# Long convolutions of a decoder layer: filter taps laid out in pairs 16 steps apart, and four buffer loads per slice in place of six

## The chip, the cores and the metric

The kernel runs on one core of a Trainium2 chip. The metric is the device time of one execution in microseconds. PE is the matrix engine, DVE the vector engine, ACT the scalar engine, POOL the general engine, SP the engine that issues most transfers.

## The reference

One decoder layer for 8 sequences of 256 tokens, width 256. Its first block makes q, k and v by projections, a 4-tap convolution and SiLU, runs a chunked delta rule with inverted triangles of 32x32, and mixes five paths per head with a gate. Three of the paths are causal depthwise convolutions of v with 3, 15 and 64 taps:

```
def _dwconv(x, w):
    K = w.shape[1]
    xt = jnp.pad(jnp.transpose(x, (0, 2, 1)), ((0, 0), (0, 0), (K - 1, 0)))
    y = jax.lax.conv_general_dilated(xt, w[:, None, :], (1,), 'VALID',
        dimension_numbers=('NCH', 'OIH', 'NCH'), feature_group_count=w.shape[0])
    return jnp.transpose(y, (0, 2, 1))
paths = jnp.stack([_dwconv(v, fir_s), _dwconv(v, fir_m), _dwconv(v, fir_l), delta_path, v], axis=3)
```

(reshapes left out). A cross attention over a second input and a mixture of experts follow; each block ends in a residual and a layer norm. All arrays are float32.

## The kernel before

The phase `phase_project_invert_and_fir` does, for 8 batches in a software pipeline (`weave`), the projections (L423), the short convolutions (ACT L499, DVE L550), the transposes (L456), norms (DVE L567, POOL L594 and L597, DVE L574) and the triangle matrices. Each engine's program is an order written out by hand; semaphores tie them. At its end come the long convolutions (`pe_fir`, `act_fir`), beside DVE's inversion of the triangles (`dve_invert`).

**How a long convolution becomes a product.** Channels are cut into 8 slices (`SLICES`) of 32 channels (`SL`). For one channel, `win` holds windows of 128 time steps of v, one for each of the 32 blocks of 64 outputs (8 batches x 4 blocks). The buffer `hank` holds for each of 3 filters (`NF`) and each of 64 steps (`BLK`) the filter shifted by that step, over 128 partitions. The product of L666 takes the 128x32 windows of one channel as weights and streams the 3 x 64 = 192 columns of `hank` for that channel. There are 256 such products, four at a time on four column groups (`q`) of the array. Each shows as two records in the trace (512), since the data are float32. Two channels (`u`) of each of the four groups make a `pair`; ACT copies a pair out of PSUM to `stage` in one instruction (L686), turned so that channels lie innermost. A slice has four pairs.

**The layout.** The buffer is `hank[k, f, s, c]`, so the columns of one channel lie 32 floats (128 bytes) apart. It is filled from a DRAM copy of the transposed filters, `rt_dram[slice, f, n, c]`, with `hank[k, f, s, c] = rt[f, k + s, c]`: partition k reads one run of consecutive rows from row k. Only ranges in which taps can be nonzero are loaded, in six transfers per slice (the tuple `HANK`, function `sp_hank`, L763 to L768); the rest stays zero from a clearing by POOL at the start (L345, 12 memsets).

**Making `rt_dram`.** The filters are loaded right-aligned to the zeroed `wpad` (L312), turned by PE (L322, 6 transposes), copied by ACT (L328, 6 copies) to `filters`, and stored by SP (L336, 8 transfers, and L339 for the rows of zeros behind).

**Order of SP.** Slices 0 to 3 are loaded during rounds 4 to 7 of the batches (`sp_first_hank`), to four buffers (`RING`). Slice n from 4 to 7 is loaded when the last product of slice n - 4 is done (`sp_late_hank`). SP then goes on in this order (`sp_first`, L914 to L927): the inverses of the first half (L608, which wait for DVE), the tokens of batches 0 and 1 (L973), the triangles of batch 0 (L983, L984, which wait for the inverses in DRAM), the stage stores of slices 0 to 3 (L614), the triangles of batch 1, the stage stores of slices 4 to 7. The next phase loads the convolved paths (L1150) after all six stage stores have landed, and then tokens of batch 2 (L973).

**Order of DVE.** The first inversion, then a fixed part of the second, then the first products of the next phase (L1115), which need tokens; L1119 needs PE's transposes of L1003, which on PE stand behind the last product of L666.

Of the kernel before, what the change touches and what calls it, by code (L numbers as in the profile page):

```python
# [226 lines left out]
HANK = ((2, 1, 0, 32), (2, 1, 32, 96), (2, 1, 96, P), (0, 2, 48, 64), (0, 2, 64, 96), (0, 2, 96, P))  # L227
# [15 lines left out]
def phase_project_invert_and_fir(pg, a, env):  # L243
# [5 lines left out]
    with ExitStack() as mem:  # L249
# [10 lines left out]
        n_stage, n_inv, n_filters = NF * BLK * CH, NG * CH * CH, KT * NF * P  # L260
# [9 lines left out]
        stage = [views(r, 0, n_stage, "p (f t c) -> p f t c", f=NF, t=BLK) for r in (room0, room1)]  # L270
# [13 lines left out]
        filters = views(room3, 0, n_filters, "p (k r f c) -> p k r f c", k=KT, r=RING, f=NF)  # L284
        wpad = views(room3, n_filters, n_filters, "p (k f n) -> p k f n", k=KT, f=NF)
        am = views(room3, 0, n_inv, "p (g i j) -> p g i j", g=NG, i=CH)
        no_taps = env.hank[0][0:BLK, 0, 0:SLICES * NF, :]
# [28 lines left out]

        def pe_filters():
            pe.wait_ge(s.wpad, 16 * NF)
            for k in range(KT):
                for f in range(NF):  # L320
                    n = k * NF + f
                    m = nc.tensor.transpose(ps[:, 6 + n // 4, n % 4 * P:(n % 4 + 1) * P], wpad[:, k, f, :], ident[:])  # L322
            m.then_inc(*s.filters_turned.up())

        def act_filters():
            act.wait_ge(s.filters_turned, 1)
            for n in range(KT * NF):
                S.copy(filters[:, n // NF, :, n % NF, :].rearrange("n r (q c) -> n q r c", q=NCH),  # L328
                       ps[:, 6 + n // 4, n % 4 * P:(n % 4 + 1) * P].rearrange("n (q r c) -> n q r c", q=NCH, r=RING)
                       ).then_inc(*s.filters_copied.up())  # L330

        def sp_filters():
            sp.wait_ge(s.filters_copied, KT * NF)
# [7 lines left out]
        def pool_hank_zero():  # L341
            for h in env.hank:
                for f in range(NF):
                    pool.in_turn()
                    G.memset(h[:, f].rearrange("k s c -> k (s c)"), 0.0).then_inc(*pool.tick(env.hank_zero))  # L345
# [62 lines left out]
        def pe_project(b):  # L408
# [37 lines left out]
        def pe_normalise(b):  # L446
            for j in range(3):
# [3 lines left out]
                else:  # L451
                    pe.wait_ge(s.win_made, b)
                    pe.wait_ge(s.filters_copied, KT * NF)
# [58 lines left out]
        def act_normalise(b):  # L512
# [7 lines left out]
            act.wait_ge(s.tok_out[i], 16 * (b // 2))  # L520
            S.copy(tok[i][:, :, 2, :], ps[:, 6, :].rearrange("p (t d) -> p t d", t=TT)).then_inc(*s.v_copied.up())
# [41 lines left out]
        def dve_normalise(b):  # L563
# [7 lines left out]
            dve.wait_ge(s.tok_out[i], 16 * (b // 2))  # L571
# [187 lines left out]
def sp_hank(pg, env, sl):  # L759
# [3 lines left out]
    for f, count, k0, k1 in HANK:  # L763
# [5 lines left out]
        if k1 == P:  # L769
            yield  # L770
# [1974 lines left out]
```

## Time and profile before

| | us |
|---|---|
| median of 3 runs | 985.71 (980.92 to 992.03) |
| the profiled execution, its own time | 989.73 |
| its span in the trace | 987.9 |
| PE busy | 880.9 (89% of the span) |
| DVE busy | 605.2 (61%) |
| ACT busy | 453.4 (46%) |
| products of the long convolutions (L666), 512 records | 44.7 |

Busy times are sums over the span; matrix instructions overlap, and busy time counts the overlap once. An engine that is busy need not be the one that sets the end: for this, the stretch from 120 to 205 us has to be read, in which the long convolutions end and the next phase begins. The granted clock of PE is 0.95 of full speed on average over the span.

### The profile page before, as it was taken

How to read it: one execution, taken by the hardware profiler on the slowest of the kernel's cores; microseconds unless marked ns; L12 is line 12 of the kernel's file. 1: busy time of each engine (PE TensorE's matmuls, PEld its weight loads, DVE VectorE, ACT ScalarE, POOL GpSimd, SP SyncE). 2: the span in 40 equal slices, each digit the busy share in tenths (PEclk: the TensorE clock that was granted, in tenths of full speed). 3: DMA queues.
4: the chain of work that ended last, by engine and by line, in shares of the span. 5: the costliest groups of instructions: out<-in, count | busy, mean ns of one | idle time of the engine just before them, and what ended most of it. 6: DMA issues, size and time to landing. Idle time of an engine off the chain costs nothing.

```text
span 987.9 us, 18338 instructions
## 1 busy us (share of the span) xinstructions
PE 880.9 (89%) x6859; PEld 656.0 (66%) x6859; DVE 605.2 (61%) x1409; ACT 453.4 (46%) x845; POOL 342.9 (35%) x334
## 2 busy tenths in 40 slices
PE   7799789889999988898889888989997999999995
PEld 5667566667777766687556555656785777777774
DVE  5799798566888887452657767774462343333255
ACT  5687665446666664443144543445331322222221
POOL 9422201023556555331001343223540242222683
PEclk9899999768999997899799999999998999999998
DMA  5689769996455431121992112002302222221421
GB/s 169 186 276 276 205 169 258 285 238 152 108 116 114 82 76 54 53 86 70 387 375 93 63 63 87 11 23 87 92 23 82 65 56 64 65 67 49 150 65 64
DMA packets 144396, 123.52 MB, mean 125 GB/s; under 512 B 89718, under 2 KB 126518, under 8 KB 143030
## 3 DMA queue, kind: packets, MB, share of 16 engines
q1 hardware_dynamic: 140902, 112.98, 40.3%
q0 software_dynamic: 3408, 9.38, 2.5%
q8 instruction: 56, 0.92, 0.4%
q14 instruction: 30, 0.25, 0.1%
HBM read 74.04 MB, written 48.29 MB: 124 GB/s over the span
## 4 chain that ended last, share of the span: by engine, by line
PE 60%; DVE 13%; ACT 10%; POOL 8%; issue 4%; DMA 3%; SPq 2%; POOLq 0%; DVEq 0%; ACTq 0%; another core or an unknown queue 0%
PE ps L2498 10%; PE ps L1904 6%; PE ps L2513 5%; PE ps L666 4%; DVE cross_room L1937 4%; PE ps L2362 3%; PE ps L1844 3%; PE ps L1605 2%; PE ps L2375 2%; PE ps L1338 2%; POOL hank L345 2%; PE ps L1966 2%; POOL kept L2645 2%; PE ps L423 2%; PE ps L1489 2%
## 5 line engine op out<-in xcount | busy, mean ns | idle before, releaser
L1982 ACT ACTIVATE cross_room<-ps 128x1024 f32<-128x1024 f32 x64 | 65.5, 1023 | 99.3 <-PE ps L1908 94.8
L2498 PE MATMUL ps<-wr,xbT 128*128 x312 | 100.4, 465 | 1.8 <-ACT xbT L2534 1.8
L1937 DVE TENSOR_REDUCE cross_room<-ps 128x4 f32<-128x1024 f32 x64 | 78.0, 1223 | 38.5 <-PE ps L1904 37.7
L1904 PE MATMUL ps<-kept,cross_room 32*128 32x256 f32 x512 | 73.3, 407 | 21.7 <-DVE cross_room L1937 20.1
L2587 POOL DMA_INDIRECT y_dram<-yb,dest_row x39 | 37.4, 960 | 136.4 <-DVE dest_row L2563 132.2
L1306 POOL TENSOR_TENSOR st<-st,exponent 128x20 f32<-128x20 f32 x16 | 56.5, 3533 | 66.1 <-DVE st L1281 64.8
L2498 PEld LDWEIGHTS ps<-wr,xbT 128*128 128x128 f32 x312 | 59.3, 191 | 30.1 <-issue 3.5
L1908 PE MATMUL ps<-cross_room,kept 32*128 32x256 f32 x512 | 74.5, 409 | 0.0
L1904 PEld LDWEIGHTS ps<-kept,cross_room 32*128 32x128 f32 x512 | 46.5, 188 | 39.6 <-issue 22.9
L550 DVE SCALAR_TENSOR_TENSOR room<-room 128x256 f32<-128x256 f32 x144 | 58.3, 478 | 11.6 <-ACT room L499 11.6
L2572 DVE TENSOR_TENSOR cross_room<-cross_room,ps 128x352 f32<-128x352 f32 x39 | 20.3, 521 | 60.3 <-PE ps L2498 58.9
L2542 ACT ACTIVATE cross_room<-ps 128x352 f32<-128x352 f32 x39 | 18.1, 463 | 73.4 <-PE ps L2498 73.4
L2578 DVE TENSOR_SCALAR yb<-ps,weight 128x256 f32<-128x256 f32 x39 | 18.9, 484 | 50.5 <-PE ps L2513 50.5
L423 PE MATMUL ps<-room,weights 128*128 128x256 f32 x192 | 46.6, 395 | 3.4 <-DMA room<-in_conv_v 2.7
L666 PE MATMUL ps<-hank,win 128*32 128x192 f32 x512 | 44.7, 513 | 5.0 <-issue 2.7
L1281 DVE TENSOR_REDUCE st<-paths 128x20 f32<-128x1280 f32 x32 | 47.1, 1476 | 0.0
L1908 PEld LDWEIGHTS ps<-cross_room,kept 32*128 32x128 f32 x512 | 44.7, 188 | 1.8 <-issue 1.4
L423 PEld LDWEIGHTS ps<-room,weights 128*128 128x128 f32 x192 | 37.0, 200 | 9.1 <-DMA room<-in_conv_v 3.1
L666 PEld LDWEIGHTS ps<-hank,win 128*32 128x32 f32 x512 | 30.6, 150 | 18.2 <-issue 5.5
L2432 POOL TENSOR_TENSOR hTlo<-cross_room,hThi 128x512 fp32r<-128x512 f32 (+1 forms) x24 | 31.1, 1298 | 30.7 <-ACT hThi L2391 29.5
L1338 PE MATMUL ps<-dxT,w1x 128*128 128x256 f32 x128 | 38.2, 426 | 2.9 <-ACT stT L1362 2.9
L2362 PE MATMUL ps<-x2Thi,whi 128*128 128x512 f32 (+1 forms) x96 | 38.6, 403 | 0.6 <-issue 0.6
(350 smaller groups left out, 2253.8 us busy)
## 6 DMA issues: line engine op xcount, KB each, us to landing
xs_dram<-params SPq DMA_DIRECT2D x17, 1040.0 KB, 17.9
room<-in_gW SPq DMA_DIRECT2D x8, 1280.0 KB, 8.4
tok_dram<-room SPq DMA_DIRECT2D x8, 768.0 KB, 5.9
fir_dram<-room SPq DMA_DIRECT2D x6, 1024.0 KB, 7.2
paths<-fir_dram SPq DMA_DIRECT2D x48, 128.0 KB, 3.7
xb<-xs_dram SPq DMA_DIRECT2D x39, 130.0 KB, 2.4
hank<-rt_dram SPq DMA_DIRECT2D x8, 512.0 KB, 7.9
yr<-y_dram SPq DMA_DIRECT2D x16, 256.0 KB, 3.3
```

The source lines that it names most:

```text
L423: m = nc.tensor.matmul(ps[:, 1 + j, c * T:(c + 1) * T], W[j][:, k, c * P:(c + 1) * P], xT[:, k, :], start=(k == 0), stop=(k == KT - 1))
L550: V.scalar_tensor_tensor(out=conv[:, j, c, :], in0=raw[:, j, c, tap:tap + T], scalar=taps[:, j, c, tap:tap + 1], in1=conv[:, j, c, :], op0 ...
L666: m = nc.tensor.matmul(ps[q * CH:(q + 1) * CH, sl % 2 * PAIRS + pair, u * NF * BLK:(u + 1) * NF * BLK], win[:, sl // RING, :, q * CH + in_ ...
L1306: G.tensor_tensor(st[:, t, 3].rearrange("p n h -> p (n h)"), st[:, t, 1].rearrange("p n h -> p (n h)"), env.exponent[:, 1, 0:NPATH * H], A ...
L1338: m = nc.tensor.matmul(ps[:, 6 + c // 2, (c % 2) * T:(c % 2 + 1) * T], w, xT[:, k, :] if k < KT else stT[:], start=(k == 0), stop=(k == KT))
L1904: m1 = nc.tensor.matmul(ps[:, c, t * T:(t + 1) * T], strips(qS[b % 3], g, c)[:, t * P:(t + 1) * P], kS(b, g)[c * CH:(c + 1) * CH], start=T ...
L1908: m2 = nc.tensor.matmul(ps[:, c, t * T:(t + 1) * T], kS(b - 1, g)[c * CH:(c + 1) * CH, t * P:(t + 1) * P], strips(qS[(b - 1) % 3], g, c), ...
L1937: V.tensor_reduce(mx[:, :, g, XD + 2 * h * CH:XD + (2 * h + 1) * CH + 1:CH].rearrange("p t c -> p c t"), ps[:, pair(h), :].rearrange("p c ...
L1982: S.activation(pT[g % 2][:, pair(h)].rearrange("p c k t -> p (c k t)"), ps[:, pair(h), :].rearrange("p c n -> p (c n)"), ACT.Exp).then_inc ...
L2362: m = nc.tensor.matmul(ps[0:fn, 2 * par + j, :], w[a_][:, j, k, f0:f0 + fn], env.x2T[b_][:, k, tg * TG:(tg + 1) * TG], start=(k, a_, b_) = ...
L2498: m = nc.tensor.matmul(ps[:, 2 * (j % 2) + half, 0:FF], xbT[j % 2][:, k, :], wr[:, bass.ds(e, 1), k, half, :].rearrange("p e n -> p (e n)" ...
L2513: m = nc.tensor.matmul(ps[:, 5 + j % 2, 0:D], hbT[j % 2][0:fn, n, :], wdr[n][0:fn, bass.ds(e, 1), :].rearrange("p e n -> p (e n)"), start= ...
```

## The change

The buffer and its DRAM copy are laid out anew. A period of 32 steps (`PER`) is cut in two halves of 16 (`LAG`), and steps t and t + 16 lie side by side: `hank[k, a, f, i, c, h]` holds step `32a + 16h + i`. In DRAM a row of 64 floats holds for each of 32 channels the tap of row n and the tap of row n + 16. So a product streams 96 pairs of adjacent floats, pairs 64 floats (256 bytes) apart; the columns stay 192, in another order.

The filters are turned twice, once shifted by 16 (12 transposes, 12 copies in place of 6 and 6), and `wpad` is 16 columns wider. PE writes the turned filters to banks 6, 7 and 3 and therefore waits for the first batch's raw copies; the third projection of batch 1 waits for the copies of the filters. `filters` moves to the second token buffer, so ACT's and DVE's writes of batch 1's tokens wait for the filter stores to have landed. Rows of the filter stores are 256 bytes, not 128.

A slice is loaded in four transfers: filter 2 over partitions 32 to 127 for the first half of the steps and 0 to 95 for the second; filters 0 and 1 over 80 to 127 and 48 to 95. Every run is 4,096 bytes. `stage` is laid out as [2 halves, 3 filters, 32 steps, 32 channels], so a stage store has two runs of 4 KB per partition, not one of 8 KB, in the same six transfers. The copy of L686 moves the same 384 elements in the new order.

```diff
-HANK = ((2, 1, 0, 32), (2, 1, 32, 96), (2, 1, 96, P), (0, 2, 48, 64), (0, 2, 64, 96), (0, 2, 96, P))
+LAG = 16
+PER = 2 * LAG
+STEPS_A = BLK // PER
+HANK = ((2, 1, 0, 32, P), (2, 1, 1, 0, 96), (0, 2, 0, 80, P), (0, 2, 1, 48, 96))
...
+        def filter_bank(n):
+            return ps[:, (6, 7, 3)[n // 4], n % 4 * P:(n % 4 + 1) * P]
...
+            pe.wait_ge(s.raw_copied, 3)
+            for n in range(FILTERS):
+                h, k, f = n // (KT * NF), n // NF % KT, n % NF
+                m = nc.tensor.transpose(filter_bank(n), wpad[:, k, f, h * LAG:h * LAG + P], ident[:])
...
+                S.copy(filters[:, k, :, f, h::2].rearrange("n r (q c) -> n q r c", q=NCH),
+                       filter_bank(n).rearrange("n (q r c) -> n q r c", q=NCH, r=RING)).then_inc(*s.filters_copied.up())
...
+                if j == 2 and b == 1:
+                    pe.wait_ge(s.filters_copied, FILTERS)
...
+            if b == 1:
+                act.wait_ge(s.filters_out, FILTERS_OUT)
...
+            if b == 1:
+                dve.wait_ge(s.filters_out, FILTERS_OUT)
...
-                nc.sync.dma_start(env.fir_dram[f, c * NCH:(c + 1) * NCH].rearrange("q (n t) d -> (q n) (t d)", t=BLK),
-                                stage[c][:, f].rearrange("p t d -> p (t d)")).then_inc(*env.fir_out.up(16))
+                nc.sync.dma_start(env.fir_dram[f, c * NCH:(c + 1) * NCH].rearrange("q (n a t) d -> (q n) a (t d)", a=STEPS_A, t=PER),
+                                stage[c][:, :, NF - 1 - f].rearrange("p a t d -> p a (t d)")).then_inc(*env.fir_out.up(16))
...
-                                                 env.hank[sl % RING][:, :, :, q * SL // NCH + pair * 2 + u].rearrange("k f s -> k (f s)"),
+                                                 env.hank[sl % RING][:, :, :, :, q * SL // NCH + pair * 2 + u].rearrange("k a f i h -> k (a f i) h"),
...
-                    S.copy(stage[sl // RING].rearrange("p f t c -> p c f t")[:, c0:c0 + 2, :, ::-1],
-                           ps[:, sl % 2 * PAIRS + pair, 0:2 * NF * BLK].rearrange("p (c f t) -> p c f t", c=2, f=NF)
+                    S.copy(stage[sl // RING].rearrange("p a f (h i) c -> p c (a f) i h", h=2)[:, c0:c0 + 2, ::-1, ::-1, ::-1],
+                           ps[:, sl % 2 * PAIRS + pair, 0:2 * NF * BLK].rearrange("p (c n i h) -> p c n i h", c=2, i=LAG, h=2)
...
+    for f, count, step, k0, k1 in HANK:
+        row = 2 * SL
+        src = bass.AP(tensor=rt.tensor, offset=((sl * NF + f) * (P + BLK) + PER * step + k0) * row,
+                      ap=[[row, k1 - k0], [(P + BLK) * row, count], [1, LAG * row]])
+        nc.sync.dma_start(env.hank[sl % RING][k0:k1, step, f:f + count].rearrange("k f i c h -> k f (i c h)"),
+                          src).then_inc(*env.hank_in[sl % RING].up(16))
+        if step:
+            yield
...
-        env.rt_dram = nc.dram_tensor("rt_dram", [SLICES, NF, P + BLK, SL], F32).ap()
+        env.rt_dram = nc.dram_tensor("rt_dram", [SLICES, NF, P + BLK, 2 * SL], F32).ap()
...
-            env.hank = [mem.enter_context(nc.sbuf_tensor(f"hank{i}", [P, NF, BLK, SL], F32)) for i in range(RING)]
+            env.hank = [mem.enter_context(nc.sbuf_tensor(f"hank{i}", [P, STEPS_A, NF, LAG, SL, 2], F32)) for i in range(RING)]
```

## Rows read from the trace of the kernel before

**Rows 1.** Chain of waits, 118 to 240 us: start us, length us, what.
```profile
129.19 41.68 PE ps L666 x437
...
180.71 9.68 DMA fir_dram<-room
...
195.94 5.85 DMA delta_room<-tok_dram
```

**Rows 2.** PE groups by shape: count, busy us, mean ns of one, idle before.
```profile
L666 PE MATMUL ps<-hank,win 128*32 128x192 f32 x512 | 44.7, 513 | 5.0 <-issue 2.7 <-DVE room L584 2.3
...
L1966 PE MATMUL ps<-cross_room 128*32 128x256 f32 x512 | 35.1, 393 | 2.6 <-ACT cross_room L1982 2.6
```

**Rows 3.** Lines L666, L423, L456: ns min/median/max, first and last start us.
```profile
L666 PE MATMUL ps<-hank,win x512: 500/500/599, 120.1 to 170.4; 128*32 128x192 f32 x171
...
L423 PE MATMUL ps<-room,weights x192: 377/378/796, 7.7 to 109.5; 128*128 128x256 f32 x192
...
L456 PE MATMUL ps<-ident,room x96: 271/273/477, 19.0 to 117.2; 128*128 128x128 f32 x96
```

**Rows 4.** Stretches: length, busy of PE, PEld, DVE, ACT, POOL, clock, DMA share, GB/s.
```profile
60.00:110.00 50.00, 44.20 (x300) 34.76 (x298) 45.94 (x104) 38.86 (x77) 12.40 (x8) 1.00 1.02 284
...
138.00:162.00 24.00, 24.00 (x286) 16.73 (x282) 21.70 (x62) 18.60 (x25) 1.94 (x2) 1.00 1.03 217
162.00:167.00 5.00, 5.00 (x60) 3.41 (x56) 4.64 (x11) 2.88 (x4) 0.00 (x0) 1.00 1.02 410
...
206.97:229.70 22.73, 22.17 (x213) 17.22 (x213) 13.57 (x24) 7.49 (x21) 7.07 (x2) 0.50 0.90 203
```

**Rows 5.** Timeline of SP's transfer issues: start us, length us, line, what, count.
```profile
27.14 0.70 SPq L339 DMA_DIRECT2D rt_dram<-hank  x1
...
133.77 17.76 SPq L767 DMA_DIRECT2D hank<-rt_dram  x24
151.57 0.90 SPq L608 DMA_DIRECT2D t_dram<-room  x2
...
178.89 3.78 SPq L614 DMA_DIRECT2D fir_dram<-room  x3
```

**Rows 6.** SP's waits, 120 to 200 us: total us, times, longest us.
```profile
SPq L69 <- DMA t_dram<-room: 13.0, 1, 13.0
...
SPq L767 <- PE ps L666: 5.6, 3, 2.3
```

**Rows 7.** Timeline of DVE, 118 to 200 us: idle before and releaser in brackets.
```profile
124.17 0.91 DVE L625 MEMSET room<- 128x1024 f32 x1 [0.16 <-issue]
...
169.15 0.69 DVE L1115 TENSOR_TENSOR kept<-delta_room,beta 128x512 f32<-128x512 f32 x1 [0.37 <-DMA delta_room<-tok_dram]
172.46 0.69 DVE L1119 COPY kept<-ps 128x512 f32<-128x512 f32 x1 [2.62 <-PE ps L1003]
```

**Rows 8.** Timeline of ACT in the long convolutions.
```profile
137.60 2.69 ACT L686 COPY room<-ps 128x384 f32<-128x384 f32 x4
```

**Rows 9.** Timelines of POOL, ACT and DVE in the first 50 us.
```profile
5.75 22.30 POOL L345 MEMSET hank<- 128x2048 f32 x12
...
20.62 1.08 ACT L328 COPY room<-ps 128x128 f32<-128x128 f32 x6
...
42.65 0.56 ACT L521 COPY room<-ps 128x512 f32<-128x512 f32 x1
...
32.05 1.29 DVE L574 TENSOR_TENSOR room<-ps,room 128x512 f32<-128x512 f32 x2 [3.11 <-POOL room L597]
```

**Rows 10.** Timeline of PE at four places.
```profile
101.50 0.66 PE L404 MATMUL ps<-ident,room 128*128 128x128 f32 x4 [1.25 <-DMA room<-in_x]
...
190.06 1.14 PE L1025 MATMUL ps<-kept 64*128 64x96 f32 x16
...
201.83 0.66 PE L1003 MATMUL ps<-ident,delta_room 128*128 128x128 f32 x4 [1.01 <-DMA delta_room<-tok_dram]
...
208.12 2.03 PE L1025 MATMUL ps<-kept 64*128 64x96 f32 x16
```

More of the change, by code:

```diff
@@ L269, in phase_project_invert_and_fir @@
         xT = views(room1, n_raw + 2 * n_tok + 2 * n_x, n_x, "p (k t) -> p k t", k=KT)
-        stage = [views(r, 0, n_stage, "p (f t c) -> p f t c", f=NF, t=BLK) for r in (room0, room1)]
+        stage = [views(r, 0, n_stage, "p (a f t c) -> p a f t c", a=STEPS_A, f=NF, t=PER) for r in (room0, room1)]
         room2 = sb("room2", [P, 2 * n_inv])
@@ L283, in phase_project_invert_and_fir @@
         room3 = sb("room3", [P, n_inv])
-        filters = views(room3, 0, n_filters, "p (k r f c) -> p k r f c", k=KT, r=RING, f=NF)
-        wpad = views(room3, n_filters, n_filters, "p (k f n) -> p k f n", k=KT, f=NF)
+        filters = tok[1].rearrange("p t j d -> p (t j d)").rearrange("p (k r f c) -> p k r f c", k=KT, r=RING, f=NF)
+        wpad = views(room3, 0, n_wpad, "p (k f n) -> p k f n", k=KT, f=NF)
         am = views(room3, 0, n_inv, "p (g i j) -> p g i j", g=NG, i=CH)
-        no_taps = env.hank[0][0:BLK, 0, 0:SLICES * NF, :]
+        no_taps = views(env.hank[0][0:BLK].rearrange("k a f i c h -> k (a f i c h)"), 0, SLICES * NF * 2 * SL, "k (n c) -> k n c", n=SLICES * NF)
+        FILTERS, FILTERS_OUT = 2 * KT * NF, 16 * (KT * RING + 1)
         gw1_rows = a["gW1"][D:, :].rearrange("(n g p) c -> p g n c", n=NPATH, p=P)
@@ L326, in act_filters @@
             act.wait_ge(s.filters_turned, 1)
[L327 to L330, printed above, removed]
+            for n in range(FILTERS):
+                h, k, f = n // (KT * NF), n // NF % KT, n % NF
+                S.copy(filters[:, k, :, f, h::2].rearrange("n r (q c) -> n q r c", q=NCH),
+                       filter_bank(n).rearrange("n (q r c) -> n q r c", q=NCH, r=RING)).then_inc(*s.filters_copied.up())
         def sp_filters():
-            sp.wait_ge(s.filters_copied, KT * NF)
+            sp.wait_ge(s.filters_copied, FILTERS)
             for k in range(KT):
@@ L344, in pool_hank_zero @@
                     pool.in_turn()
-                    G.memset(h[:, f].rearrange("k s c -> k (s c)"), 0.0).then_inc(*pool.tick(env.hank_zero))
+                    G.memset(h[:].rearrange("k a f i c h -> k (a f i c h)")[:, f * BLK * SL:(f + 1) * BLK * SL], 0.0).then_inc(*pool.tick(env.hank_zero))
         def sp_first_hank(sl):
@@ L452, in pe_normalise @@
                     pe.wait_ge(s.win_made, b)
-                    pe.wait_ge(s.filters_copied, KT * NF)
+                    pe.wait_ge(s.filters_copied, FILTERS)
                 for t in range(TT):
@@ L762, in sp_hank @@
     nc, rt = pg.nc, env.rt_dram
-    for f, count, k0, k1 in HANK:
-        s0, s1 = max(0, P - FIRS[f + count - 1] - k1 + 1), min(BLK, P - k0)
-        src = bass.AP(tensor=rt.tensor, offset=((sl * NF + f) * (P + BLK) + s0 + k0) * SL,
-                      ap=[[SL, k1 - k0], [(P + BLK) * SL, count], [1, (s1 - s0) * SL]])
-        nc.sync.dma_start(env.hank[sl % RING][k0:k1, f:f + count, s0:s1, :].rearrange("k f s c -> k f (s c)"),
+    for f, count, step, k0, k1 in HANK:
[3 more added lines that the diff above has]
+        nc.sync.dma_start(env.hank[sl % RING][k0:k1, step, f:f + count].rearrange("k f i c h -> k f (i c h)"),
                           src).then_inc(*env.hank_in[sl % RING].up(16))
-        if k1 == P:
+        if step:
             yield
```

6 lines of the change are left out of this document (1 added, 5 removed).

## The prediction

> **What bounds the kernel now.** I read the chain of waits around the long convolutions first. One piece of 41.68 us, the products of L666, runs from 129.19 us to the end of the stage, and two transfers stand behind it: the stores to `fir_dram` that let SP go on at 190.4, and the token load issued then, whose landing starts products at 201.83 [rows 1], for which PE had idled 1.01 us [rows 10]. So three chains have to be separated: PE, the transfers, DVE.
>
> **PE.** A float32 product is two records in the trace. L666 streams 192 columns, 128 bytes from one to the next, and its record lasts 500 ns at the median. L423 with 256 columns side by side lasts 378, the transpose of L456 with 128 lasts 273 [rows 3]: 105 ns per 128 columns, so 192 should last 325. The excess, 175, is about a second time the 160 that 192 columns cost by this slope: the spread columns are read at half rate. L1966 has the same 128x32 weights in four column groups and 256 columns side by side: 68.6 ns of engine time per record (35.1/512) against 87.3 (44.7/512) for L666 [rows 2].
>
> **Transfers.** From 138 to 162 us the queues are full (share 1.03) and move only 217 GB/s, while in 162 to 167, where whole 128-partition loads and stores pass, they move 410 [rows 4]. In the full stretch it is the `hank` loads of slices 4 to 7: 4 x 1,444 KB = 5.91 MB at 217 GB/s is 27.3 us, from their first issue at 133.77 [rows 5] to about 161.5. SP waited for PE before three of these slices, 5.6 us in all [rows 6]. Behind them queue the inverses, issued at 151.57 when DVE has them [rows 5], and the tokens. SP then waits 13.0 us for the inverses to land [rows 6], and only then issues the triangles and the stage stores of L614, the second half at 178.89 [rows 5]. The order of SP thus makes the store wait for the last `hank` load, not for the last product.
>
> **DVE.** It inverts triangles from 124.17 to 168.8 in a fixed order, and its first work of the next phase starts at 169.15, after 0.37 us lost on the token load; then it waits 2.62 us for PE's L1003 [rows 7]. That 2.6 is all that an earlier end of L666 can give here.
>
> **The change, part by part.**
>
> *Products.* Each now reads 96 pairs of neighbours, pairs 256 bytes apart. No row has pairs. The lower bound of the time is L1966's per column, 68.6 x 192/256 = 51.5 ns per record, 26.4 us in all; the upper is no gain, 44.7. I take full rate, between 51.5 and the 68.6 that the nearest row needs as it stands [rows 2]: 26.4 to 35.1 us, so PE saves 10 to 18 us of its 44.7, and a slice takes 3.3 to 4.4 us instead of 5.6. The row that decides is the excess of 175 ns, which goes if two reads share what one pays for.
> The Trainium skill (SBUF — State Buffer, Specifications (TRN2)) says that the memory has 16-byte lines and needs two hits in a line for full bandwidth. By this rule one float in a line is slow and the pair is enough, and a record would last 325 ns. The 500 ns agree with its first half; no run here shows the second.
>
> *Late slices.* The old transfers of a slice are, from the ranges in the code, 124, 512, 128, 56, 368 and 256 KB, the 512 over 64 partitions, the others over 16 or 32; the new ones are 384 KB each, two over 96 partitions and two over 48: 1,536 KB, 6% more. Their price is unknown. All at 410 GB/s, a slice takes 3.84 us against 6.81 now, -11.9 us for four; all at 217, 7.25, +1.7. But 217 is a mean of wide and narrow: if the 64-partition load alone ran at 410 (524 kB in 1.28 us), the narrow 954 kB took 5.53, which is 173 GB/s. With the new narrow half (786 kB) at 173 and the wide half at only 217, a slice takes 4.55 + 3.62 = 8.17, +5.4 for four: the upper end. I take the wide half at 410, as 96 partitions are nearest to the full ones, and the narrow at 173: 1.92 + 4.55 = 6.47, -1.4 for four. The start moves too: faster PE frees the buffers earlier, and slice 5, for which SP waited on PE, can be issued some 2 us earlier. Of this I count 1.5, since slice 4 stays where SP puts it, at 133.77. Last load: 2.9 us earlier, about 158.6.
> By the Trainium skill (SBUF — State Buffer, Door 1: The DMA port swizzle) a transfer within 32 or 64 partitions reaches half of the ports. An estimate from its table gives the old slice 1.7 times the time per byte of full width, near the 410/217 = 1.9 of the rows, and the new one 1.5 to 1.7: by it four slices take 2.2 us less to 0.8 more, and the gain below would be 0.8 to 3.5.
>
> *End of the stage.* PE waits for slice 7 and does it in 3.3 to 4.4: its end moves from 171 to about 163. DVE then saves its 2.6, no more. Late next is the chain of transfers: inverses, triangles, stores of 6 MB, paths, tokens, all 2.9 us earlier. At 201.83 PE had lost 1.01 us on the tokens [rows 10]; coming 2.5 us earlier it could use them 3.5 earlier, and gets them 2.9 earlier. **Gain: 2.9 us.** Even if the transfers gave more, 2.5 + 1.0 = 3.5 is the limit here.
>
> *Evacuation.* The 32 copies of L686 keep 384 elements. Four in a row take 2.69, 0.67 each [rows 8]; against 16 x 51.5 ns = 0.82 of PE per copy, ACT is just enough, with three table loads beside it. Other strides on the write side: 0 to +0.2 us each. I take 0, as the old ones jump already 128 bytes between elements, and +0.2 x 32 = 6.4 would still end before slice 7's load; for slice 7 alone it is +0.8. PE may run 8 copies ahead.
>
> *Stage stores.* The same 6 transfers and bytes, in pieces of 4 KB, not 8. The 410 GB/s of [rows 4] were moved mostly in 4 and 6 KB rows, so 0.
>
> *First half.* Six more transposes on PE, six more copies on ACT (1.08 for six now, at 20.62), a `wpad` memset larger by 96 columns. The copies delay the square, the DVE sum and the raw copies behind them by 1.1 us. What hides it: POOL clears `hank` until 28.05 and only then takes the sum; DVE waits 3.11 us for POOL's power [rows 9]. If the clearing were 3 us shorter, the 1.1 would be on the path. PE waits newly for these copies at batch 1's third projection, some 2 us after their end, with all later products behind it: 0. The memset is on the path: at 22.30/12 us for 2,048 columns [rows 9], 96 cost +0.1. SP issues the nine filter transfers 1.1 later, in rows of 256 bytes, not 128, and behind them the loads of a batch. They are all issued by 27.84 [rows 5], and the new waits on them, ACT's L521 and DVE's L574 of batch 1, come first at 42.65 [rows 9]: some 14 us of cover for twice the bytes, so 0. If it went, each engine would stop with the rest of batch 1 behind it. Slices 0 to 3 load beside the projections, at share 1.02 [rows 4]: by the same price -0.3 per slice, which nobody waits for but the load of `in_x` at 101.50 (1.25 us, [rows 10]); I take 0, the upper end is +1.36 per slice. SP issues two transfers less per slice, 17.76/24 = 0.74 us each with their waits [rows 5]: beside other work, 0.
>
> **Sum.** -2.9 + 0.1 = -2.8. The profiled execution took 989.73 (span 987.9 and 1.8 around it), 4.0 above the median of 985.71; its gaps are taken as the median's. 989.73 becomes 986.9, and the median 982.9: **983**.
>
> **Rivals.**
> *A, the narrow loads set the pace (slower).* Half of the new bytes go to 48 partitions,. At 8.17 us per slice the late loads end 5.4 - 1.5 = 3.9 later, the tokens at 169 and 201.83 with them, and each early slice adds up to 1.36 to a full queue: +3.9 to +9.3, 990 to 995. It decides once a slice takes over 7.2 us. For: 65% of the old bytes were narrow and made 217 of 410; against: now 50% are. Chance 0.17.
> *B, transfers relieved.* Towards 410 the last `hank` lands before the inverses leave DVE; gain 3.5 plus the 1.25 at 101.50: 981. Chance 0.15.
> *C, the pairs do nothing.* Records stay at 500 ns and PE ends as now; the transfers alone give -1.0 to +5.4: 985 to 991. For: no row has pairs. Chance 0.08.
> *D, the clock.* From 206.97 to 229.70 PE is granted 0.50, its lower level of 1.2 GHz, after it had idled [rows 4]; the sixteen records of L1025 take 2.03 us there and 1.14 a batch earlier [rows 10]. With all of its 22.7 us scaled so, the stretch costs 9.9, with nothing 0; I take 6.6, since DVE, busy for 13.6 of it, does not get faster. PE will now idle in the convolutions, waiting for loads, and a stretch may come or go: -6.6 or +6.6 with the rest, 976 or 990. Chance 0.1 each way.
> The Trainium skill (TensorE: Matmul & The Clock Gate, HAM oscillation) says that stalls between bursts of products put the engine back to the slow clock; by it the new idle time would sooner cost a stretch, the 990 above.
>
> The forecast itself has 0.4, with 980 to 987 as its own range. Together, low 975 (B with D) and high 993 (most of A). A measurement here tells about 1% (9.9 us) from no change. Faster by that needs B and D together, -3.5 - 1.3 - 6.6, or luck in both medians: 0.15. Slower by that, A with D: 0.11. Within: 0.74.
>
> **What would show it.** Right: L666's records at about 325 ns, 51 to 69 ns of engine time each, PE idle at L666 with `hank` loads as releaser, DVE's wait at L1119 near 0, tokens at about 200. Wrong, if records stay at 500 (C); if the rate between 138 and 158 is under 210 GB/s (A) or over 300 (B); if ACT's L686 passes 1 us; if ACT or DVE wait for `rt_dram` near 42; if `fir_dram` lands later than 190.

## The result, and the profile after

The kernel became slower: 992.11 us at the median of 20 runs (987.63 to 1000.03) against 983.34 of the kernel before in the same session, a ratio of 1.0093 [1.0071, 1.0115]. The forecast was 2.8 us less than before. Rival A, the loads that set the pace, came true.

| at, us | before | after | later by |
|---|---|---|---|
| convolutions start | 129.19 | 133.11 | 3.9 |
| last product of theirs ends | 170.9 | 176.4 | 5.5 |
| DVE starts the next step | 169.15 | 176.06 | 6.9 |
| tokens of the batch behind are issued | 195.94 | 203.50 | 7.6 |
| DVE takes these tokens | 201.81 | 210.33 | 8.5 |
| span | 987.9 | 996.6 | 8.7 |

All of the loss is there by 210: from there to the end both profiled executions take 786 us. Line 666 of before is L681 after, 686 is L701, 767 is L782, 1115 is L1130, 608 is L623, 614 is L629, and 973 is L988.

The products did what the diff says. Of L681 by form, as in [rows 2], and of the line alone, as in [rows 3]:

```profile
L681 PE MATMUL ps<-hank,win 128*32 128x192 f32 x512 | 33.4, 430 | 16.8 <-DMA hank<-rt_dram 11.8 <-issue 2.7 <-DVE room L599 1.9
```

```profile
L681 PE MATMUL ps<-hank,win x512: 322/444/552, 123.4 to 176.1; 128*32 128x192 f32 x171
```

The shortest record is 322 ns where none was under 500. The median is 444 since a good part of them ran at a lower clock. PE's timeline of after shows it (start, length, idle before and its releaser):

```profile
103.20 0.66 PE L413 MATMUL ps<-ident,room 128*128 128x128 f32 x4 [2.51 <-DMA room<-in_x]
...
129.16 2.08 PE L488 MATMUL ps<-room 64*128 64x128 f32 x16 [0.68 <-ACT room L547]
133.11 9.37 PE L681 MATMUL ps<-hank,win 128*32 128x192 f32 x160 [1.88 <-DVE room L599]
142.87 2.95 PE L681 MATMUL ps<-hank,win 128*32 128x192 f32 x64 [0.40 <-ACT room L701]
148.30 4.43 PE L681 MATMUL ps<-hank,win 128*32 128x192 f32 x64 [2.48 <-DMA hank<-rt_dram]
157.12 5.13 PE L681 MATMUL ps<-hank,win 128*32 128x192 f32 x64 [4.38 <-DMA hank<-rt_dram]
165.00 4.56 PE L681 MATMUL ps<-hank,win 128*32 128x192 f32 x64 [2.76 <-DMA hank<-rt_dram]
171.77 4.61 PE L681 MATMUL ps<-hank,win 128*32 128x192 f32 x64 [2.21 <-DMA hank<-rt_dram]
```

A slice is 64 records: 2.95 us at 142.87, 46 ns each, where it took 5.6. From 148 on every slice waits for its load, and the starts are 8.8, 7.9 and 6.8 us apart, 7.8 on average. The one long piece of [rows 1] has broken up in the chain of waits (start, length, what):

```profile
147.17 24.57 DMA hank<-rt_dram
...
171.77 3.91 PE ps L681 x48
...
190.71 7.85 DMA fir_dram<-room
...
203.50 6.82 DMA delta_room<-tok_dram
```

The stretches (columns as in [rows 4]): the queues are full and move 208 GB/s, less than the 217 of before, and PE is granted 0.77. In the earlier stretch, share 1.02 has become 1.06.

```profile
60.00:110.00 50.00, 42.88 (x282) 33.34 (x281) 43.41 (x97) 36.14 (x71) 9.34 (x7) 0.97 1.06 282
...
142.00:172.00 30.00, 17.77 (x270) 12.37 (x266) 27.27 (x75) 20.15 (x29) 1.91 (x2) 0.77 1.04 208
```

SP's waits from 120 to 200 us, against [rows 6]: it no longer waits long for PE, and waits 17.2 us for the inverses to land behind the loads.

```profile
SPq L69 <- DMA t_dram<-room: 17.2, 1, 17.2
...
SPq L782 <- PE ps L681: 2.6, 3, 1.6
```

SP's timeline, against [rows 5]: the late loads are out in 9.96 us instead of 17.76, but the stores of the second half, which it issues after that wait, leave 8.05 us later.

```profile
137.64 9.96 SPq L782 DMA_DIRECT2D hank<-rt_dram  x16
...
154.58 1.43 SPq L623 DMA_DIRECT2D t_dram<-room  x2
...
177.28 3.61 SPq L629 DMA_DIRECT2D fir_dram<-room  x3
...
186.94 4.41 SPq L629 DMA_DIRECT2D fir_dram<-room  x3
...
203.50 0.55 SPq L988 DMA_DIRECT2D delta_room<-tok_dram  x1
```

DVE, against [rows 7], now idles on both token loads: 3.35 us where it was 0.37, and 4.34 where it was 1.73. ACT's copies are as before, 0.67 each, as in [rows 8].

```profile
176.06 0.69 DVE L1130 TENSOR_TENSOR kept<-delta_room,beta 128x512 f32<-128x512 f32 x1 [3.35 <-DMA delta_room<-tok_dram]
...
210.33 0.69 DVE L1130 TENSOR_TENSOR kept<-delta_room,beta 128x512 f32<-128x512 f32 x1 [4.34 <-DMA delta_room<-tok_dram]
```

```profile
141.96 2.70 ACT L701 COPY room<-ps 128x384 f32<-128x384 f32 x4
```

### The profile page after: what moved, and what is told of

The parts are those of the page before. It is cut to its first block, busy times and chain, and to the rows that moved or that the text cites. A ratio compares the mean times of both kernels' runs of the same rounds, so it can differ in the third digit from the quotient of the medians.

```text
span 996.6 us, 18343 instructions
## 1 busy us (share of the span) xinstructions
PE 874.7 (88%) x6865; PEld 652.8 (66%) x6865; DVE 605.4 (61%) x1409; ACT 453.1 (45%) x851; POOL 344.4 (35%) x334
## 4 chain that ended last, share of the span: by engine, by line
PE 56%; DVE 12%; ACT 11%; POOL 7%; DMA 6%; issue 4%; SPq 2%; POOLq 0%; DVEq 0%; ACTq 0%; another core or an unknown queue 0%
PE ps L2513 9%; PE ps L1919 6%; PE ps L2528 5%; PE ps L2377 3%; DVE cross_room L1952 3%; PE ps L1859 3%; DMA hank<-rt_dram 2%; PE ps L1620 2%; PE ps L1981 2%; PE ps L1353 2%; POOL hank L354 2%; POOL kept L2660 2%; PE ps L2390 2%; PE ps L434 2%; PE ps L1504 2%
## 5 line engine op out<-in xcount | busy, mean ns | idle before, releaser
L1997 ACT ACTIVATE cross_room<-ps 128x1024 f32<-128x1024 f32 x64 | 65.5, 1024 | 99.7 <-PE ps L1923 97.4
L681 PE MATMUL ps<-hank,win 128*32 128x192 f32 x512 | 33.4, 430 | 16.8 <-DMA hank<-rt_dram 11.8
L1923 PEld LDWEIGHTS ps<-cross_room,kept 32*128 32x128 f32 x512 | 45.7, 192 | 1.8 <-issue 1.4
L681 PEld LDWEIGHTS ps<-hank,win 128*32 128x32 f32 x512 | 24.1, 162 | 25.6 <-DMA hank<-rt_dram 13.3
```

The costliest lines, as they stand in the source:

```text
L681: m = nc.tensor.matmul(ps[q * CH:(q + 1) * CH, sl % 2 * PAIRS + pair, u * NF * BLK:(u + 1) * NF * BLK], win[:, sl // RING, :, q * CH + in_ ...
L1923: m2 = nc.tensor.matmul(ps[:, c, t * T:(t + 1) * T], kS(b - 1, g)[c * CH:(c + 1) * CH, t * P:(t + 1) * P], strips(qS[(b - 1) % 3], g, c), ...
L1997: S.activation(pT[g % 2][:, pair(h)].rearrange("p c k t -> p (c k t)"), ps[:, pair(h), :].rearrange("p c n -> p (c n)"), ACT.Exp).then_inc ...
```

## The experiments

Theory N says that the loads into few partitions are slow by their shape; its rival S, that rows which overlap in DRAM are. Then: why do the pairs gain nothing where no load is in the way?

**1. The source rows.** Each partition reads rows of its own from an input instead of rows that overlap those of its neighbours. Same destinations, same bytes.

```diff
-        src = bass.AP(tensor=rt.tensor, offset=((sl * NF + f) * (P + BLK) + PER * step + k0) * row,
-                      ap=[[row, k1 - k0], [(P + BLK) * row, count], [1, LAG * row]])
+        src = bass.AP(tensor=own.tensor, offset=(sl % RING * HANK_DMAS + HANK.index((f, count, step, k0, k1))) * 96 * run,
+                      ap=[[count * run, k1 - k0], [run, count], [1, run]])
```

> The changed kernel, but each partition of a buffer load reads 4 KB of its own from the gate's weights in DRAM, not overlapping rows of the filter copy (the convolutions get other taps). Destinations, sizes and order of the transfers stay. Theory N (narrow): the 48-partition transfers set the pace whatever they read, so the late slices stay at about 8 us each, 205 to 215 GB/s, and the time within 0.3% of the changed kernel (992). Theory S (shared source): all partitions reading one region of 48 KB is what is slow, so the rate rises towards the 400 GB/s of the token loads, a slice takes about 4 us, the wait of the inverses on SP shrinks from 17 to under 8 us, and the time falls to 980 to 984.

987.1 us, 1.0072 [1.0037, 1.0107]; the slices are 7.2 us apart instead of 7.8. One thing more changed with the rows: the two short filters' runs of a partition now lie side by side in the source as well, and part of the packets are 8 KB where all were 4 KB. So the 0.6 us belongs to both.

> The kernel before with the same edit: rows of its own for every partition, same destinations, sizes and order. Theory N: 217 GB/s in the late loads as before. Theory S: towards 400 GB/s, the last buffer load lands by about 150 instead of 162.

985.93 in a single run. The full stretch moves more, 248 GB/s for 217, still far from 410:

```profile
138.00:162.00 24.00, 24.00 (x293) 20.84 (x291) 21.70 (x62) 18.76 (x25) 1.93 (x2) 1.00 1.03 248
```

Overlap in the source has at most a small part, 0.6 us of a slice. S is not the main cause.

**2. The width.** `HANK` alone is changed, the list of each slice's transfers: (first filter, filters, step, first partition, end). Of after:

```diff
 HANK = ((2, 1, 0, 32, P), (2, 1, 1, 0, 96), (0, 2, 0, 80, P), (0, 2, 1, 48, 96))   # changed kernel, 1,536 KB
+HANK = ((2, 1, 0, 0, P),  (2, 1, 1, 0, P),  (0, 2, 0, 0, P),  (0, 2, 1, 0, P))     # full_width, 3,072 KB
+HANK = ((2, 1, 0, 0, P),  (2, 1, 1, 0, P),  (0, 2, 0, 80, P), (0, 2, 1, 32, 96))   # wide_long, 1,920 KB
+HANK = ((2, 1, 0, 0, P),  (2, 1, 1, 0, P),  (0, 2, 0, 0, P),  (0, 2, 1, 32, 96))   # wide_three, 2,560 KB
```

> The changed kernel with all four transfers of a slice over 128 partitions (3,072 KB per slice, twice the bytes; the result is unchanged). Theory N: full width moves 400 GB/s, so a slice takes 7.9 us, as the 8.2 of the changed kernel, and the time stays within 3 us of it. Theory S: 3.1 MB at 208 GB/s are 15 us per slice, the last late load lands some 28 us later, and the time is over 1,015.

> The changed kernel with the two transfers of the 64-tap filter over all 128 partitions (512 KB each, not 384) and the second one of the short filters over 32 to 95 (512 KB, not 384), so that only one narrow transfer is left; 1,920 KB per slice, 25% more. Theory N (narrow): 1.28 us for each of the three at 410 GB/s and 2.2 to 2.4 for the narrow one, 6.1 us per slice against 8.2 now, so the last load lands at 162 or earlier and the time is 982 to 986, 6 to 9 us below the changed kernel. Theory B (bytes at 210 GB/s): 9.3 us per slice and slower than the changed kernel by 4.

> As wide_long, and the first transfer of the short filters over all 128 partitions as well (1,024 KB, not 384): 2,560 KB per slice, no narrow one. Theory N: 6.4 us per slice, equal to wide_long or 1 us slower, 983 to 987. If the transfer over 80 to 127 costs more than its share of ports explains, this one is the faster.

full_width: 998.3 in a single run. Twice the bytes take the changed kernel's time per slice, 7.7 us, at twice the rate:

```profile
142.00:170.00 28.00, 17.12 (x256) 11.60 (x249) 25.41 (x71) 18.99 (x27) 2.58 (x2) 0.76 1.03 408
```

wide_long: 987.64, 1.0045 [1.0015, 1.0075], 7.5 us per slice. wide_three: 982.36, 1.0018 [0.9987, 1.0049], 6.6 us per slice. The rows are wide_long's and then wide_three's stretch:

```profile
142.00:166.00 24.00, 15.38 (x244) 10.85 (x236) 21.70 (x62) 18.04 (x26) 1.90 (x2) 0.79 1.03 265
```

```profile
142.00:166.00 24.00, 14.58 (x244) 11.23 (x240) 21.73 (x61) 17.61 (x25) 1.90 (x2) 0.86 1.03 411
```

They differ in one transfer, into partitions 80 to 127 or into all. 640 KB more make the slice shorter by 0.9. If the other three run at 408 (512 KB in 1.28 us each), the one into 80 to 127 takes 7.5 - 3.85 = 3.7 us for 393 kB, 107 GB/s. So N's direction is right, and here one transfer costs half of the slice. It is not the whole of the changed kernel's price: of its 7.8 us the other three loads have 4.1 left for 1,180 kB, 288 GB/s and not 408.

**3. How narrow, or where.** Wide_three has a transfer into 64 partitions, 32 to 95, and its mean of 411 leaves no room for a slow one. If 64 are fast, the big one may be 64 wide too:

```diff
+HANK = ((2, 1, 0, 0, P),  (2, 1, 1, 0, P),  (0, 2, 0, 64, P), (0, 2, 1, 32, 96))   # even64, 2,048 KB
+HANK = ((2, 1, 0, 32, P), (2, 1, 1, 0, 96), (0, 2, 0, 64, P), (0, 2, 1, 32, 96))   # trim64, 1,792 KB
```

> wide_three (982.4 us, 1.0018) with the transfer into all 128 partitions of 1,024 KB narrowed to partitions 64 to 127: 128, 128, 64 and 64 partitions, 2,048 KB per slice. Theory N (it is the transfers into 48 partitions that are slow; the ones into 64, of which wide_three has one, run at the full 408 GB/s): a slice takes 5.14 us (2.10 MB / 408) instead of 6.6, the last load lands about 5 us earlier, SP's wait for the inverses falls from 11.6 to under 8, the stores of the stage and the tokens come up to 2.5 us earlier, and VectorE (no idle time from 124.2 to 169.15 before) becomes the bound: ratio 0.996 to 1.000. Rival W (only the full width is fast, 64 partitions run at half, 205 GB/s): the two of 512 KB take 2.56 each, a slice 7.7 us, ratio 1.005 to 1.009.

> even64 with its two wide transfers back on the 96 partitions of the changed kernel: 96, 96, 64 and 64 partitions, 1,792 KB. It differs from the changed kernel by the two of 48 partitions alone. Theory N (the 48 are the fault, 96 cost nothing extra): a slice takes 4.5 us at 408 GB/s, time as even64 within 1 us or less. Rival (96 partitions are slow too): rate at 250 to 330 GB/s, a slice 5.6 to 7.3 us, ratio 1.002 to 1.007.

even64: 992.16, 1.0102 [1.0072, 1.0132]; trim64: 994.84, 1.0145 [1.0081, 1.0209]. Both of my theories missed: N expected 5.1 us, its rival 7.7. PE's timeline of even64:

```profile
147.97 3.13 PE L681 MATMUL ps<-hank,win 128*32 128x192 f32 x64 [2.00 <-DMA hank<-rt_dram]
157.36 5.37 PE L681 MATMUL ps<-hank,win 128*32 128x192 f32 x64 [6.26 <-DMA hank<-rt_dram]
168.14 5.33 PE L681 MATMUL ps<-hank,win 128*32 128x192 f32 x64 [5.41 <-DMA hank<-rt_dram]
175.05 2.96 PE L681 MATMUL ps<-hank,win 128*32 128x192 f32 x64 [1.58 <-DMA hank<-rt_dram]
```

9.0 us from one slice to the next, with half a megabyte less than wide_three. Taken as before, 524 kB into partitions 64 to 127 would cost 9.0 - 3.85 = 5.2 us. That is too much, since in these 27.08 us the queues moved more than the slices:

```profile
147.97:175.05 27.08, 13.83 (x193) 8.68 (x193) 22.91 (x63) 14.38 (x20) 1.90 (x2) 0.75 1.03 289
```

At 289 GB/s that is 7.8 MB, and three slices have 6.3. The rest belongs to the inverses and tokens issued behind them: the core's 16 DMA engines get out of step, and those that are ahead go on to the next transfers while PE waits for the last one. (Slice 6 has 64 landing events; the last but one comes at 165.0, the last at 168.1.) The three slices' own bytes need 21.8 us at this rate, 7.3 each, and so the load into 64 to 127 about 7.3 - 3.85 = 3.4 us, 150 GB/s, where the same bytes into 32 to 95 go at full rate. By the same working (286 GB/s, 6.9 a slice) the load into 80 to 127 of wide_long takes 3.0, not 3.7. All of these are estimates by subtraction. The stretches of even64 swing with its loads:

```profile
150.00:154.00 4.00, 1.10 (x26) 0.75 (x16) 3.62 (x12) 3.99 (x8) 1.90 (x2) 1.00 1.03 196
154.00:158.00 4.00, 0.64 (x8) 0.43 (x12) 3.47 (x11) 1.71 (x3) 0.00 (x0) 0.78 1.05 345
```

Those of trim64 do not. It has even64's two narrow loads and 96 partitions in place of 128 in the others, a quarter of a megabyte less, and takes 8.0 us a slice. Of its six stretches of 4 us from 148 to 172 none is above the second of these two:

```profile
164.00:168.00 4.00, 1.74 (x24) 1.13 (x28) 3.69 (x10) 0.14 (x1) 0.00 (x0) 0.63 1.06 222
168.00:172.00 4.00, 3.64 (x48) 1.81 (x40) 3.69 (x10) 2.68 (x4) 0.00 (x0) 0.51 1.02 238
```

With 3.4 for the load above 64 and 1.28 for the one across it, its two loads of 96 partitions took 3.3 us, 240 GB/s, where 128 partitions go at 408 and more bytes take 2.6. So the rival of trim64 had the direction ("96 partitions are slow too") and too small a size. The number of partitions decides nothing here: 64 of them across partition 64 are at full rate, 64 above it at about 150 GB/s, and 96 in between. No run has loads of 96 without one above 64 beside them, and none has a load wholly below 64, so neither is shown by itself.

The Trainium skill (SBUF — State Buffer, Door 1: The DMA port swizzle) says that the partition's bit of 64 chooses between the two ports of a cluster, so 64 to 127 reach 8 of 16 ports and 32 to 95 all of them. That 64 to 127 is the slow one of these two is as that rule has it. Its size is not: by half the ports 64 to 127 would take about what all 128 take, 2.6 us, and even64 would need wide_three's 6.4 us for a slice; here it needed 7.3.

**4. The same without the pairs.** The kernel before, with two full loads per slice:

```diff
-HANK = ((2, 1, 0, 32), (2, 1, 32, 96), (2, 1, 96, P), (0, 2, 48, 64), (0, 2, 64, 96), (0, 2, 96, P))
+HANK = ((2, 1, 0, P), (0, 2, 0, P))
```

> The kernel before, no pairs, with each slice's six transfers replaced by two into all 128 partitions: 1,536 KB per slice instead of 1,444, same output. In even64 a transfer into partitions 64 to 127 made a slice 9 us where wide_three, with that one over 0 to 127, needs 6.6; and wide_three has a fast one into 64 partitions, 32 to 95. Theory H (what is slow is a transfer whose partitions lie on one side of 64, not a narrow one as such; before has four of its six so): 138 to 150 moves 400 GB/s or more, a slice takes 3.9 us, no wait for hank anywhere, t_dram 13.0 goes under 5, the input load's 1.25 at 101.50 goes; products stay at 500 ns and end their chain at 170 to 171 as now, VectorE bounds the stage, so ratio 0.995 to 0.999, the fastest of all. Rival R (the 4 KB rows that overlap by 128 bytes in DRAM are what is slow, 217 GB/s): 215 to 260 GB/s, time as before or 1 us more.

987.73, 1.0068 [1.0037, 1.0099]. I had the bytes wrong by two: the loads are 1,024 and 2,048 KB, 3,072 per slice. (And five of before's six loads lie on one side of 64, not four.) The rate is as expected and rival R falls, with rows that overlap all the same:

```profile
142.00:162.00 20.00, 20.00 (x241) 16.26 (x233) 18.02 (x53) 16.20 (x22) 1.92 (x2) 1.00 1.01 422
```

At 422 GB/s these bytes take 7.5 us per slice, more than the 6.8 of before. Speed per byte was bought with bytes, and theory H's time, priced on half of them, is missed.

**5. No late loads.** Slices 4 to 7 use what slices 0 to 3 left, in either kernel:

```diff
-                pe.wait_ge(env.hank_in[sl % RING], 16 * HANK_DMAS * (sl // RING + 1))
+                pe.wait_ge(env.hank_in[sl % RING], 16 * HANK_DMAS)
...
-            for sl in range(RING, SLICES):
-                env.sp_late_hank(sl)
```

> The changed kernel without the loads of slices 4 to 7: those slices use the taps of slices 0 to 3 again. This leaves the products and takes the late transfers away. If the pairs do what the trace says (2.95 us per slice at full clock against 5.4), the convolutions end by about 157, but DVE inverts until 168.8 + 3, so against nolate_before the time falls by 2 to 5 us only. If the clock lost in the convolutions was part of the price of the changed kernel, it stays at 1.00 up to 150 here.

> The kernel before without the loads of slices 4 to 7. The products keep their 500 ns and end at about 170, as in the kernel before, since PE hardly waited for loads. The inverses land about 10 us earlier, so the stage stores of slices 0 to 3 go out by 160 and the time is 1 to 4 us under the kernel before.

nolate_after: 986.91, 1.0034 [1.0011, 1.0057]. nolate_before: 980.59, 0.9977 [0.9948, 1.0006]. With all late loads gone the pairs are still the slower kernel, by 6.3 us. 4.2 of it is the start of the convolutions, 133.66 against 129.50, and 1.6 that DVE reaches the next step 41.0 us after it, not 39.4. From its first work on the inverses to that step DVE hardly waits. nolate_before's timeline:

```profile
124.46 0.91 DVE L625 MEMSET room<- 128x1024 f32 x1 [0.16 <-issue]
...
168.90 0.67 DVE L1113 TENSOR_TENSOR kept<-delta_room,beta 128x512 f32<-128x512 f32 x1
```

44.4 us, and 45.0 in the kernel before, 124.17 to 169.15. This is the bound of the stage, and none of it waits for a product of the convolutions.

**6. The early loads.** They could go one round earlier, alone or with wide_three's list:

```diff
-        weave([sp_fetch, sp_project, sp_normalise], B, {2: sp_filters}, {4 + sl: sp_first_hank(sl) for sl in range(RING)})
+        weave([sp_fetch, sp_project, sp_normalise], B, {2: sp_filters}, {3 + sl: sp_first_hank(sl) for sl in range(RING)})
```

> The changed kernel with the loads of slices 0 to 3 one batch round earlier (rounds 3 to 6, about 42 to 92 us, where the queues are less full than from 60 to 110). Theory E (the early loads are a part of the loss): the batch whose x waits behind slice 3 no longer does, the convolutions start at 130 instead of 133, and the time falls by 2 to 4 us to 988 to 990. Theory L (only the late loads cost): no change, 992.

> The kernel before with the early loads one round earlier: it lost 1.25 us on x at 101.50. 981 to 983, 0 to 2 us less than before. It shows how much of early_wide's time comes from the move of the loads and not from the pairs.

> wide_three (all transfers over 64 or 128 partitions, none on one side only) with the early loads one round earlier. Late slices at 6.6 us each as in wide_three, start of the convolutions at 129 instead of 130.6: 979 to 983, 1 to 3 us under the kernel before. If PE's half clock after the idle time in the convolutions weighs more, no gain: 983 to 985.

early_after 992.98, 1.0108 [1.0069, 1.0147]; early_before 986.1, 1.0029 [0.9994, 1.0065]; early_wide 985.71, 1.0015 [0.9981, 1.0048]. No gain: in early_after PE waits 4.56 us for `in_x` at 93.06 instead of 2.51 at 103.20. The round moves the collision, it doesn't end it.

**7. Pairs with nothing in the way.** No late loads, early round, wide_three's list:

> early_wide without the loads of slices 4 to 7 (those slices use the taps of slices 0 to 3 again): what the pairs give when no transfer is in their way. Products in 2.95 us per slice, ended by 158. Against nolate_before (980.6) the time is 976 to 979 if an early end of the convolutions is worth DVE's 2.6 us, and 980 to 983 if PE's idle time up to DVE's end at 169 costs it the clock afterwards.

983.47, 1.0011 [0.9975, 1.0048]. The products end at 156.3, 14 us before those of nolate_before, and the kernel is no faster than before. Its DVE and then its stretch from 160:

```profile
124.72 0.91 DVE L640 MEMSET room<- 128x1024 f32 x1 [0.16 <-issue]
...
171.35 0.69 DVE L1128 TENSOR_TENSOR kept<-delta_room,beta 128x512 f32<-128x512 f32 x1
172.07 0.69 DVE L1132 COPY kept<-ps 128x512 f32<-128x512 f32 x1
174.10 0.69 DVE L1137 COPY kept<-ps 128x512 f32<-128x512 f32 x1 [1.34 <-PE ps L1016]
```

```profile
160.00:170.00 10.00, 1.09 (x4) 0.72 (x4) 9.24 (x23) 0.30 (x1) 0.00 (x0) 0.50 1.01 346
```

The wait of 2.62 us for PE, at the copy that is L1132 here, is gone, as the prediction says. What it gave is lost again in two places. DVE works 46.6 us, 2.2 more than in nolate_before: 0.5 is a wait for PE's products of L488, which last 2.08 us at a granted clock of 0.50 (1.16 in nolate_before), its operations of L652 last 378 ns at the mean instead of 362, and its copy 1.57 us instead of 1.13. Behind that it waits 1.34 us at the next copy. So from its first work on the inverses to this copy it takes 49.4 us, and 49.2 in the kernel before. PE hardly works for 10 us and is granted 0.50. The longer work is no chance of one run: without waits for tokens it is 45.7 to 46.7 us in five other runs with pairs, and 44.4 to 44.6 in before, own_before and nolate_before.

**8. Is it the clock?** The products of slices 4 to 7 (to 6 in wide_fill and after_fill) are issued twice, so that PE idles less:

```diff
-                    for u in range(2):
+                    for again in range(2 if 4 <= sl < 8 else 1):
+                      for u in range(2):
```

> nolate_early_wide (983.5 us, 1.0011; slices 4 to 7 use the buffers that slices 0 to 3 filled, so half of the convolution reads wrong taps) with the products of slices 4 to 7 issued twice: 256 products more, 11.8 us of TensorE at full clock. In nolate_early_wide TensorE's products are done at 156.3, VectorE works until about 169, and the granted clock is 0.50 to 0.67 from 160 to 190. Theory C: with the doubled products TensorE is busy until about 168, the clock from 160 to 190 is 0.9 or more, the steps behind the convolutions run at full speed and the distance from the convolutions' start to the second copy of the last step's VectorE (70.0 us there) falls by 3 to 6 us: time 977 to 981, below nolate_early_wide although it does more work. Rival T: the distance stays at 69 to 71 or grows, the time 983 to 986.

> wide_three (982.4 us, 1.0018 of the kernel before) with the products of slices 4 to 6 issued twice, 192 products more, same output. TensorE waits 2 to 3.5 us for each of these slices' buffers there, and works at a granted clock of 0.72 to 0.85. Theory C (the rest of the pairs' gain is lost in the clock, which falls while TensorE stands idle): the clock in the stretch of the convolutions and the 10 us behind them is at 0.9 or more, the chain ends 1 to 4 us earlier, ratio 0.996 to 1.000. Rival T (the pace is the transfers' and the clock plays no part): the slices stay 6.4 to 6.6 us apart, the doubled products fill the waits, the time is the same within 1 us of wide_three, 1.000 to 1.003. If the doubled products run at half clock (4.4 us per 64) they take 8.8 us per slice and set the pace themselves: ratio over 1.005.

> The changed kernel with the products of slices 4 to 6 issued twice, same output. Slices come 7 to 8.8 us apart there by the transfers. Theory C: the clock in the convolutions rises from 0.77 to 0.9 or more and 1 to 3 us of the 9 lost come back (ratio 1.006 to 1.008 where the changed kernel has 1.0093). Rival T: the transfers alone set the end, the time stays at 1.0093 within 0.001.

> even64 with the products of slices 4 to 7 issued twice, same output, to keep TensorE from idling. In wide_fill that put the clock to 1.00 and 0.98 in 160 to 180 and the second copy of the next step (187.59, wide_three 189.54) 2 us earlier, after which 5.6 us were lost on the token load. Theory C+N: with the transfers 5 us earlier the token load is no longer late, and the 2 us stay: ratio 0.993 to 0.998, 1 to 2 us under even64. Rival: the tokens are still late, since they queue behind the second half's stage stores, which wait for VectorE and for ScalarE's last copy: even64's time, or above.

nolate_fill: 981.86, 0.9976 [0.9944, 1.0008], against 1.0011 for nolate_early_wide: the intervals overlap, so this alone settles nothing. It also reached the convolutions 3.8 us later than nolate_early_wide, with the same program up to there, so I compare distances from their start. Its stretch and its DVE:

```profile
160.00:170.00 10.00, 9.39 (x225) 9.03 (x216) 9.14 (x26) 7.22 (x8) 0.49 (x2) 1.00 0.94 288
```

```profile
175.02 0.68 DVE L1129 TENSOR_TENSOR kept<-delta_room,beta 128x512 f32<-128x512 f32 x1
```

The clock is back at 1.00 from 160 to 170, and DVE still reaches the next step 40.8 us after the convolutions' start at 134.18 (41.0 without the filling). So the clock is not why this stage doesn't get shorter. From 170 to 190 it was 0.66 and 0.65 all the same, so theory C was not put to the test behind the stage.

wide_fill: 983.53, 0.9993 [0.9969, 1.0018]; here the clock is worth something and it is lost at once. DVE of wide_three, then of wide_fill:

```profile
189.54 0.69 DVE L1139 COPY kept<-ps 128x512 f32<-128x512 f32 x1 [3.54 <-PE ps L1018]
...
201.98 0.69 DVE L1130 TENSOR_TENSOR kept<-delta_room,beta 128x512 f32<-128x512 f32 x1 [1.64 <-DMA delta_room<-tok_dram]
```

```profile
187.59 0.69 DVE L1140 COPY kept<-ps 128x512 f32<-128x512 f32 x1 [2.63 <-PE ps L1019]
...
204.10 0.69 DVE L1131 TENSOR_TENSOR kept<-delta_room,beta 128x512 f32<-128x512 f32 x1 [5.59 <-DMA delta_room<-tok_dram]
```

At a clock of 1.00 and 0.98 from 160 to 180 (0.85 and 0.83 in wide_three) it is 2 us earlier at 187.59, and then waits 5.59 us for tokens. after_fill: 993.36, 1.0108 [1.0064, 1.0151], from four runs; even64_fill: 993.12, 1.011 [1.006, 1.0161], as even64. The medians show no gain from the clock where the loads set the pace, but the interval of after_fill also holds the 1.006 to 1.008 that theory C expected. In the profiled executions the way from the start of the convolutions to the third step's tokens is shorter with the filling, 74.2 us for 77.2 and in even64 77.9 for 79.9. Whether the clock gives something back there stays open.

No version was faster than the kernel before by more than its interval; with the whole computation, wide_three, early_wide and wide_fill come to parity with it.

## Why the prediction was wrong

- **The products: right.** "I take full rate": 322 ns for 325. Engine time was 46 ns, under my lower bound of 51.5, and a slice 2.95 us where I had 3.3 to 4.4.
- **The late slices: the step that failed.** "I take the wide half at 410, as 96 partitions are nearest to the full ones, and the narrow at 173: 1.92 + 4.55 = 6.47, -1.4 for four." Measured 7.8, +4.0 for four (8.17 was rival A's). The term that was mis-sized is the wide half: by the subtractions of experiment 3 its two loads took about 3.3 us, not 1.92. The narrow half came to about the 4.5 that I had, and that was luck: its two loads are not alike, 3.0 to 3.7 us into 80 to 127 and the rest, 0.8 to 1.5, into 48 to 95. I fitted one rate to a mean over six unlike transfers and sorted the new ones by width, where what counts is which partitions they reach. The 7.8 is measured; how it divides is an estimate.
- **The early slices: failed too.** "I take 0, the upper end is +1.36 per slice." The wait for `in_x` went from 1.25 to 2.51 us, and behind it PE ran at a granted clock of 0.66 from 103 to 108 (1.00 before). The convolutions started 3.9 later, of which 1.7 stood at 103.20; the rest came behind it. A stretch of lower clock behind a short wait was not in this term; what part of the rest it cost was not separated. With the changed kernel's list they start at 132.47 to 133.66 in three profiled runs (after, after_fill, nolate_after), with wide_three's list and the same first half at 130.37 to 131.15 in four, but at 134.18 in nolate_fill. So the loads are the likely cause, beside a scatter of the same size.
- **The limit of the gain: too high.** "2.5 + 1.0 = 3.5 is the limit here" took DVE's work in the stage to stay as long as it was. The 2.62 us at L1119 went, as said (experiment 7), but DVE's own work got 2.2 us longer beside the pairs, and 1.34 us of waiting came up behind. So without any late load the pairs were at 1.0011, with nothing gained, where this term had 3.5 us. No rival priced it.
- **The start of the late loads:** they were issued without the long waits for PE, as said (2.6 us for 5.6), but from 137.64, not 133.77, since the stage began later.
- **ACT's copies, the first half:** 0 and +0.1 predicted; 0 and +0.24 (59.79 for 59.55 at the same work) measured.
- **What followed:** "the chain of transfers [...] all 2.9 us earlier" came with the other sign. The order of SP passed 5.5 us of late products on as 8.5: the tokens queue behind the loads (DVE's 3.35), and the stores behind the inverses' landing.
- **The clock (D):** it fell, to 0.77 in the convolutions. What it cost is open: raised to 0.94 (after_fill, 142 to 172) it gave no gain that the medians show. The Trainium skill (TensorE: Matmul & The Clock Gate, HAM oscillation), which has stalls between bursts slow the engine down, agrees with the fall.

## What to carry to other kernels

A mean rate over several transfers is not the rate of any of them. Before pricing a new set, find which of the old ones are slow, and look at which partitions they reach, not at how many. Making an engine faster pays only down to the next chain with work of its own: list for each engine how long it is busy without waiting, and don't take for granted that this work stays as long beside a faster neighbour. And a buffer load that nobody waits for still fills the queue ahead of one that is waited for.

## What the runs showed of the hardware

- A load from DRAM into partitions 64 to 127 took about 3.4 us for 524 kB (even64), and one into 80 to 127 3.0 to 3.7 for 393 (wide_long), 107 to 154 GB/s; both are estimates by subtraction at 408 for the others. Into 32 to 95 it went at the full 408 to 411 (wide_three).
- Beside such a load, two into 96 partitions took about 3.3 us for 786 kB, 240 GB/s (trim64, by subtraction), where two into all 128 moved 1,049 kB in 2.6. Not tried alone.
- Rows of 8 KB that overlap in DRAM were read at 422 GB/s into all 128 partitions (before_wide), while with the old six transfers it was 217 GB/s with overlap and 248 without (own_before).
- Reading two adjacent floats per step cut the float32 product's record from 500 to 322 ns at 192 columns.
- DVE's copy of 128x1024 lasted 1.53 to 1.58 us in the three kernels with pairs and no late loads, 1.03 to 1.28 in those where PE waits for loads, and 1.13 in nolate_before, where PE has no gaps either but streams at 500 ns a record. POOL stood still beside it in nolate_early_wide. What slows it was not tried.
